# Signed feed-forward with its second layer as seven products of quarters

## The chip, the cores and the metric

One core of one Trainium2 chip runs the whole program: a decoder with two layers, each of self-attention, cross-attention and a feed-forward part. The metric is the device time of one execution in microseconds (us), as the median of the runs. All times in the tables count from the first instruction of the profiled execution.

## The reference

The last of the six stages is the one that changes. Its input x is 2 x 1024 tokens of 256 features; k0, k1 and k2 are boolean matrices of 512 x 1024, 1024 x 1024 and 1024 x 256, and s0, s1, s2 are scalars.

```python
def _L1_ffn_ref(x, k0, k1, k2, s0, s1, s2):
    def _conn_dense(kernel_bool, x):
        w = jnp.where(kernel_bool, jnp.float32(1.0), jnp.float32(-1.0))
        return x @ w
    h = jnp.concatenate([x, -x], axis=-1)
    h = s0 * _conn_dense(k0, h)
    h = jax.nn.relu(h) * 2
    h = s1 * _conn_dense(k1, h)
    h = jax.nn.relu(h) * 2
    h = s2 * _conn_dense(k2, h)
    return h
...
    x = x + _L1_ffn_ref(_layernorm(x, axis=-1), ...)
```

The stage before it is a cross-attention of 8 heads over 154 context rows for every token.

## The kernel before

The program runs stage by stage, with a barrier between stages. Only the last two stages matter here. `headed_attention` (the cross-attention) works in 21 steps on 16 tiles of 128 tokens; step s does a different part of up to five neighbouring tiles. In its spare places it prepares the signed stage: GpSimd turns k1 into +-1 weights in steps 2 to 9 (L3089, between its own `weigh_rest`, L1771, once per step), VectorE and ScalarE take the mean and variance of the first four tiles and split them into a high and a low float16 part (`Rows.low`, `Rows.high`), and TensorE turns them (`Rows.turn`, L861), ScalarE copies the turned tile out of PSUM (`Rows.copy`, L866).

`signed_ffn` works on 4 blocks of 512 tokens. All values are split in two float16 parts, whose products with the +-1 weights are added in float32 in PSUM. A block's layer 1 is 8 chunks of 128 features (4 matmuls of 512 columns each: two parts, two halves of the input), its layer 2 is 8 chunks of 16 matmuls (L3211), and its layer 3 is 4 sums over 16 matmuls of 256 columns (L3217), whose results are scaled and added to x by VectorE (L3161). After each chunk ScalarE writes the high part of the rectified sum (L3181) and VectorE the low part (L3155). The lists `ORDER` and `EARLY` fix the order on all three engines: behind chunks 4, 5 and 6 of layer 2 of a block stand the 8 chunks of layer 1 of the next, behind chunks 0 to 3 the sums of the block before, and behind chunks 2 and 3 the turning of the next block's four tiles, two at a time. GpSimd does nothing but one small power per block (L808).

Each engine takes its own instructions in the order written; a wait holds everything behind it on that engine. A wait on a semaphore stands where the code says `wait_ge`.

Of the kernel before, what the change touches and what calls it, by code (L numbers as in the profile page):

```python
# [17 lines left out]
P = 128  # L18
# [749 lines left out]
class Rows:  # L768
# [4 lines left out]
    def __init__(self, nc, ctx, signals, name, x, room):  # L773
# [8 lines left out]
        self.first = room[:, 1536:2560].bitcast(F16).rearrange("p (c n) -> p c n", c=4)  # L782
        self.s_c, self.var_ready, self.rs_ready, self.nm_ready, self.xh_ready, self.xn_ready, self.turned, self.xT_ready = (
            sem(n) for n in ("s_c", "var_ready", "rs_ready", "nm_ready", "xh_ready", "xn_ready", "turned", "xT_ready"))

    def adopt(self, later):

        self.later = later

    def block(self, b):  # L790
        return self.first if b == 0 else self.later[:, :, BT * (b - 1):BT * b]
# [927 lines left out]
def headed_attention(nc, x, ins, keys, signs, rows, opening):  # L1719
# [8 lines left out]
    with ExitStack() as ctx:  # L1728
# [34 lines left out]
        def _(g):  # L1763
# [12 lines left out]
            for s in STEPS:  # L1776
                weigh_rest(s - 1)
                if s == 2:
                    opening.power(g, 2)
                signs.on_gpsimd(g, own, s)  # L1780
                if s == 1:
                    rows.constants(g)
                if s == 10:
                    rows.power(g, 0)

        @block.vector
        def _(v):
# [41 lines left out]
            for s in STEPS:  # L1829
# [22 lines left out]
                if s in (12, 13):  # L1852
                    rows.low(v, own, s - 12)

        @block.scalar
        def _(a):
# [38 lines left out]
            for s in STEPS:  # L1895
# [1144 lines left out]
class Signs:  # L3040


    def __init__(self, nc, ctx, signals):
# [6 lines left out]
        self.id16, self.made = sb("id16", [P, P], F16), sem("made")  # L3050
# [33 lines left out]
    def on_gpsimd(self, g, own, s):  # L3084
        if 2 <= s < 2 + C1:
# [3 lines left out]
            g.tensor_scalar(self.w[1][:, c], self.k[1][:, c], self.sign2[:, 0:1], self.sign2[:, 1:2], ALU.mult, ALU.add).then_inc(self.expanded[1], 1)  # L3089

# [11 lines left out]
def signed_ffn(nc, x, ins, out, signs, rows):  # L3102


    with ExitStack() as ctx:  # L3105
# [4 lines left out]
        TPB = BT // P  # L3110
        w0, w1, w2 = signs.w
        rows.adopt(sb("xT", [P, 4, BT * (NBLK - 1)], F16))
        h1, h2 = sb("h1", [P, 2, 2, C1, BT], F16), sb("h2", [P, 2, 2, C2, BT], F16)
        BANKS = 4
        psh = ps("psh", [P, BANKS, BT])
        acc = ps("acc", [P, 4, D])
        psx = ps("psx", [P, 2, 1024], F16)
        s_v = sem("s_v")
        layer, hi_done, lo_done, summed, added, stored = (sem(n) for n in ("layer", "hi_done", "lo_done", "summed", "added", "stored"))


        ORDER, PLACE = [(1, 0, n) for n in range(C1)], {}
        EARLY = {4: (0, 1, 2), 5: (3, 4, 5), 6: (6, 7)}
        for b in range(NBLK):
            for n in range(C2):
                ORDER.append((2, b, n))
# [180 lines left out]
```

## Time and profile before

| | us |
|---|---|
| median of 3 runs (1034.52, 1038.59, 1038.72) | 1038.59 |
| profiled execution | 1034.31 |
| its span, first to last instruction | 1032.6 |
| TensorE busy with matmuls | 882.8 (85% of the span) |
| VectorE busy | 747.7 (72%) |
| ScalarE busy | 578.9 (56%) |
| GpSimd busy | 313.8 (30%) |

The page of the profile names the engines PE (TensorE matmul), PEld (its weight loads, which overlap matmuls), DVE (VectorE), ACT (ScalarE), POOL (GpSimd) and SP (the queue that issues DMAs). Busy time of PE is modelled from the starts, and neighbouring matmuls overlap. In the groups, `out<-in` are the program's names for tiles: f_h is an output of a layer (h1 or h2), f_psh and f_acc are PSUM tiles, fs_w the weights, fr_room and f_xT the turned input.

### The profile page before, as it was taken

How to read it: one execution, taken by the hardware profiler on the slowest of the kernel's cores; microseconds unless marked ns; L12 is line 12 of the kernel's file. 1: busy time of each engine (PE TensorE's matmuls, PEld its weight loads, DVE VectorE, ACT ScalarE, POOL GpSimd, SP SyncE). 2: the span in 40 equal slices, each digit the busy share in tenths (PEclk: the TensorE clock that was granted, in tenths of full speed). 3: DMA queues.
4: the chain of work that ended last, by engine and by line, in shares of the span. 5: the costliest groups of instructions: out<-in, count | busy, mean ns of one | idle time of the engine just before them, and what ended most of it. 6: DMA issues, size and time to landing. Idle time of an engine off the chain costs nothing. (4 is left out here: it accounts for less than half of the span.)

```text
span 1032.6 us, 21126 instructions
## 1 busy us (share of the span) xinstructions
PE 882.8 (85%) x8378; PEld 543.6 (53%) x8378; DVE 747.7 (72%) x1416; ACT 578.9 (56%) x1036; POOL 313.8 (30%) x294
## 2 busy tenths in 40 slices
PE   1375978897488799999689999997899988999997
PEld 0122323232256455555356777776799974455554
DVE  7899989834788889887678899875878855344412
ACT  5588789898485555453155555553788844332410
POOL 1043435322265040000266667674234110000000
PEclk9988889799588899999899999998899999999999
DMA  5403232320510030000310000000200000000001
GB/s 147 82 1 52 32 53 32 50 34 1 164 42 2 9 126 1 1 2 1 123 45 2 2 2 2 2 3 1 73 2 1 3 1 1 1 22 1 21 1 41
DMA packets 21600, 30.39 MB, mean 29 GB/s; under 512 B 5936, under 2 KB 17918, under 8 KB 20352
## 3 DMA queue, kind: packets, MB, share of 16 engines
q1 hardware_dynamic: 18752, 26.44, 11.1%
q10 hardware_dynamic: 2752, 2.62, 0.8%
q8 instruction: 67, 1.10, 0.4%
q14 instruction: 29, 0.24, 0.1%
HBM read 18.56 MB, written 2.10 MB: 20 GB/s over the span
## 5 line engine op out<-in xcount | busy, mean ns | idle before, releaser
L589 ACT ACTIVATE t_pT<-t_sc 128x1536 f32<-128x1536 f32 x96 | 136.6, 1455 | 28.2 <-PE t_sc L696 27.9
L696 PE MATMUL t_sc<-t_qk 32*128 32x512 f16 (+3 forms) x1152 | 85.8, 353 | 49.0 <-DMA t_qk<-t_sin_parts 25.7
L269 POOL TENSOR_SCALAR_AFFINE_SELECT t_pT<-t_pT 128x512 f32<-128x512 f32 x64 | 73.4, 1169 | 166.9 <-ACT t_pT L589 166.9
L3155 DVE SCALAR_TENSOR_TENSOR f_h<-f_psh,f_h 128x512 f16<-128x512 f32 x64 | 43.9, 691 | 100.8 <-ACT f_h L3181 100.7
L3211 PE MATMUL f_psh<-f_h,fs_w 128*128 128x512 f16 x512 | 114.4, 379 | 1.5 <-DVE f_h L3155 1.5
L3181 ACT ACTIVATE f_h<-f_psh 128x512 f16<-128x512 f32 x64 | 38.2, 597 | 108.4 <-PE f_psh L3211 108.4
L696 PEld LDWEIGHTS t_sc<-t_qk 32*128 32x128 f16 x1152 | 36.4, 98 | 107.4 <-issue 54.0
L717 PE MATMUL t_ot<-t_pT,t_v 128*17 128x512 f32 (+3 forms) x768 | 81.4, 535 | 12.5 <-DVE t_ou L433 5.5
L2674 POOL TENSOR_SCALAR_AFFINE_SELECT r_att<-r_att 128x1024 f16<-128x1024 f16 x64 | 69.5, 1109 | 66.4 <-DVE r_att L2714 66.3
L3211 PEld LDWEIGHTS f_psh<-f_h,fs_w 128*128 128x128 f16 x512 | 49.8, 98 | 59.0 <-issue 2.0
L1970 PE MATMUL c_pso<-ck_VO,c_pT 128*128 128x256 f16 x480 | 55.0, 273 | 1.4 <-DVE c_pT L1821 1.4
L2714 DVE TENSOR_TENSOR r_att<-r_pss,r_att 128x1024 f16<-128x1024 f32 x32 | 39.1, 1221 | 20.2 <-ACT r_att L2840 20.2
L1970 PEld LDWEIGHTS c_pso<-ck_VO,c_pT 128*128 128x128 f16 x480 | 46.3, 98 | 6.7 <-DVE c_pT L1821 1.6
L1882 ACT ACTIVATE c_pt<-c_pss,c_mx 128x154 f32<-128x154 f32 x128 | 48.5, 415 | 1.1 <-DVE c_mx L1804 1.1
L2320 PE MATMUL m_acc<-gw_down,m_hp 128*128 128x256 f16 x384 | 47.2, 273 | 1.8 <-DVE m_hp L2212 1.4
L2840 ACT CAST r_att<-r_pss 128x1024 f16<-128x1024 f32 x32 | 32.4, 1012 | 28.1 <-PE r_pss L2910 28.0
L2256 ACT ACTIVATE m_sg<-m_psg 128x512 f32<-128x512 f32 x32 | 19.1, 596 | 51.1 <-PE m_psg L2299 51.1
L2936 PE MATMUL r_psv<-ra_w,ra_xT 128*128 128x512 f16 x192 | 46.8, 380 | 1.0 <-ACT r_v L2856 1.0
L2693 POOL TENSOR_TENSOR r_sm<-r_sm,ra_sm 128x16 f32<-128x16 f32 x16 | 46.3, 2896 | 3.6 <-DVE r_sm L2755 2.0
L1771 POOL TENSOR_TENSOR c_pn<-c_pt,c_tot 128x208 f32<-128x208 f32 x16 | 23.1, 1441 | 79.5 <-DVE c_tot L1811 79.5
L717 PEld LDWEIGHTS t_ot<-t_pT,t_v 128*17 128x17 f32 x768 | 17.5, 101 | 51.7 <-issue 37.2
L2320 PEld LDWEIGHTS m_acc<-gw_down,m_hp 128*128 128x128 f16 x384 | 36.9, 98 | 12.4 <-DVE m_hp L2212 2.2
(521 smaller groups left out, 2105.6 us busy)
## 6 DMA issues: line engine op xcount, KB each, us to landing
t_qk<-t_cos_parts SPq DMA_DIRECT2D x24, 128.0 KB, 5.2
t_qk<-t_sin_parts SPq DMA_DIRECT2D x24, 128.0 KB, 6.8
x<-in_x ACTq DMA_DIRECT2D x4, 512.0 KB, 6.4
out_x<-x SPq DMA_DIRECT2D x4, 512.0 KB, 2.9
r_rcos<-in_ret_cos SPq DMA_DIRECT2D x1, 1280.0 KB, 8.8
r_rsin<-in_ret_sin SPq DMA_DIRECT2D x1, 1280.0 KB, 10.5
t_qk<-t_cos_parts SPq DMA_DIRECT2D x16, 64.0 KB, 2.6
gw_raw<-in_gateT SPq DMA_DIRECT2D x1, 1024.0 KB, 7.1
```

The source lines that it names most:

```text
L269: last = g.affine_select(out=blk, in_=blk, compare_op=ALU.is_ge, fill=0.0, base=0, pattern=[[0, 4], [1, P]], channel_multiplier=-1)
L589: a.activation(pT[:, at:at + 3, :].rearrange("p a s -> p (a s)"), sc[s % 2][:], ACT.Exp, scale=CURVE * CURVE / math.sqrt(2 * DH)).then_inc ...
L696: last = t.matmul(sc[s % 2][:, 512 * k + at:512 * k + at + w], qk[r, g % 3, 1, of_k, P * i:P * i + P], qk[r, g % 3, 0, of_q, q0:q0 + w], s ...
L717: last = t.matmul(ot[j][32 * h:32 * h + DH + 1, 512 - w:512], v1[:, b, 4 * c + h, i, :], pT[:, (4 * slot + h) % RING, at:at + w], start=be ...
L1882: last = a.activation(pt[:, q, h, :], pss[:, k, n * CTX:n * CTX + CTX], ACT.Exp, bias=mx[:, q, 3 * k + n:3 * k + n + 1], scale=1.0, accum_ ...
L1970: last = mm(pso[:, 0:D], l, r, start=(n == 0), stop=(n == len(todo) - 1))
L2320: last = mm(acc[:, j, :], hp[:, k, ph_, P * j:P * j + P], dw[:, pw, D * e:D * e + D], start=(e == 0 and j % 2 == 0 and ph_ + pw == 0), sto ...
L2674: last = g.affine_select(out=blk, in_=blk, compare_op=ALU.is_ge, fill=0.0, base=0, pattern=[[0, 8], [1, P]], channel_multiplier=-1)
L2693: g.tensor_tensor(sm[:, q, 2, :], sm[:, q, 1, :], ahead.sm[:, 4, 0:1].broadcast_to((P, HR)), ALU.pow).then_inc(pow_done, 1)
L2936: last = mm(d, l, r, start=(i == 0), stop=(i == len(todo) - 1))
L3155: v.scalar_tensor_tensor(dst[:, 1], psh[:, i % BANKS, :], 0.0, dst[:, 0], ALU.max, ALU.subtract).then_inc(lo_done, 1)
L3211: last = mm(psh[:, i % BANKS, :], l, r, start=(k == 0), stop=(k == len(todo) - 1))
```

## The change

The second layer's weight matrix is cut into 4 quarters of 512 x 512 (halves of the input features by halves of the output features), and a block's input into 4 quarters of 512 features x 256 tokens. Instead of 8 products of quarters, 7 are made, between sums of quarters (Strassen's scheme in Winograd's form). Three sums of weight quarters are made once, and one quarter is overwritten by a difference (`mixture`, by GpSimd, in steps 10 to 13 of the stage before). The sums of token quarters are made for each block by GpSimd in float32, in place (`token_sums`, 8 operations of 128 x 2 x 256 elements per block, in two sets). For them ScalarE writes layer 1's rectified output as float32 (`hf`), beside the float16 high parts of the quarters that are used as they are (`raw_high`); the sums are then split in two float16 parts by ScalarE and VectorE (`token_high`, `token_low`, 128 x 1024 elements each).

Each product is made in two units of 256 output features: 16 matmuls of 256 columns each, into one PSUM bank. p6, p7 and p4 go on in the bank in which p1 stands; between them ScalarE copies the state out as float32 (`keep_p1`, `keep_u2`, `keep_u3`), and VectorE adds p2, p5 or p3 to the copies (`sum_c11`, `sum_c22`, `sum_c12`). The four output quarters are then split as before. The order on every engine is written out: on TensorE a block b is p1 p2 of unit 0, two turns, p1 of unit 1, two turns, p2 of unit 1, p5, sums 0 and 1 of block b-1, p6, tile 0 of layer 1 of block b+1, p5 of unit 1, tile 1, p6, tile 2, p7, tile 3, p7, tile 4, p4, tile 5, p3, tile 6, p4, tile 7, sums 2 and 3 of block b-1, p3 of unit 1. The turned tiles have two places instead of one for each block. The rows of block 1 are normalised in the stage before (steps 13 to 18), those of blocks 2 and 3 in blocks 0 and 1. The output leaves in pieces of two tiles instead of four. New buffers lie in rooms of stages that are over (`keys.VO`, `keys.kT`, `keys.wq16`, `early.room`, and the boolean weights).

The core of the diff:

```diff
+        if self.alternate:
+            return self.later if b % 2 else self.first
...
+                if s in (10, 14):
+                    rows.power(g, (s - 10) // 4)
...
+                if s in (13, 14):
+                    v.wait_ge(x_done, 2 * s - 20)
+                    rows.statistics(v, own, 2 * s - 22, 2 * s - 20)
+                if s == 14:
+                    rows.spread(v, own, 1)
+                if s == 16:
+                    rows.offsets(v, 1)
+                if s in (17, 18):
+                    rows.low(v, own, s - 15)
...
+                if s in (17, 18):
+                    rows.high(a, s - 15)
...
+        todo = ((self.mix[:, 0], a(1, 0), a(1, 1), ALU.add), (self.mix[:, 1], self.mix[:, 0], a(0, 0), ALU.subtract),
+                (a(1, 0), a(0, 0), a(1, 0), ALU.subtract), (self.mix[:, 2], a(0, 1), self.mix[:, 1], ALU.subtract))
+        g.wait_ge(self.expanded[1], C1)
+        wait(g, self.mixed, n)
+        to, left, right, op = todo[n]
+        g.tensor_tensor(to, left, right, op).then_inc(self.mixed, 1)
...
+        rows.adopt(old[:, 8192:10240].rearrange("p (c n) -> p c n", c=4), True)
...
+        z, y = [ps(f"z{i}", [P, BT]) for i in range(2)], [ps(f"y{i}", [P, BT]) for i in range(2)]
+        pw, pl = ps("w", [P, BT]), ps("l", [P, BT])
+        acc, psx = ps("acc", [P, 2, D]), ps("psx", [P, 2, 512], F16)
...
+        CHUNKS = (0, 4, 1, 5, 2, 6, 3, 7)
...
+                    sp.wait_ge(added, t + 2)
+                    t0 = P * (t % (2 * TPB))
+                    sp.dma_start(out[b // 2][t0:t0 + 2 * P].rearrange("(t p) d -> p t d", p=P), x[:, t:t + 2, :]).then_inc(stored, 16)
...
+            def token_sums(b, i):
+                f, s_ = hf[i]
+                b11, b12, b21, b22 = f[:, :, 0:HT], f[:, :, HT:BT], s_[:, :, 0:HT], s_[:, :, HT:BT]
+                g.wait_ge(f_done, 8 * b + 4 * i + 4)
+                own.link(g.tensor_tensor(b11, b12, b11, ALU.subtract))
+                g.tensor_tensor(b12, b22, b12, ALU.subtract).then_inc(t_made, 1)
+                g.wait_ge(t_made, 4 * b + 2 * i + 1)
+                own.link(g.tensor_tensor(b22, b22, b11, ALU.subtract))
+                g.tensor_tensor(b21, b21, b22, ALU.subtract).then_inc(t_made, 1)
+                g.wait_ge(t_made, 4 * b + 2 * i + 2)
...
+            token_sums(0, 0)
+            token_sums(0, 1)
+            for b in range(NBLK):
+                if b + 2 < NBLK:
+                    rows.power(g, b + 2)
+                if not closing(b):
+                    token_sums(b + 1, 0)
+                    token_sums(b + 1, 1)
...
+            def token_low(b, i, j):
+                v.wait_ge(t_high, 4 * b + 2 * i + j + 1)
+                v.tensor_tensor(tm[:, b % 2, 1, i, j], hf[i][j], tm[:, b % 2, 0, i, j], ALU.subtract).then_inc(t_split, 1)
...
+            def sum_c12(u):
+                v.wait_ge(u2_kept, u + 1)
+                v.wait_ge(p3_done, u + 1)
+                v.tensor_tensor(second_kept[u % 2], second_kept[u % 2], halves(y[u % 2]), ALU.add).then_inc(c12_sum, 1)
...
+            def low(u, half, side, high, split, src):
+                v.wait_ge(high, u + 1)
+                v.scalar_tensor_tensor(out_part(u, half, side, 1), src, 0.0, out_part(u, half, side, 0), ALU.max, ALU.subtract).then_inc(split, 1)
...
+            for b in range(NBLK):
+                u0, u1 = UNITS * b, UNITS * b + 1
+                if b:
+                    sum_c12(u0 - 1)
+                    low_c12(u0 - 1)
+                token_low(b, 1, 0)
+                sum_c11(u0)
+                token_low(b, 1, 1)
+                low_c11(u0)
+                sum_c11(u1)
+                low_c11(u1)
+                if b:
+                    add(b - 1, 0, acc)
+                if b + 2 < NBLK:
+                    rows.statistics(v, own, TPB * (b + 2), TPB * (b + 3))
+                if not closing(b):
...
+                low_c12(u0)
+                if not closing(b):
+                    raw_low(b + 1, 6)
+                    token_low(b + 1, 0, 1)
+                low_c21(u1)
+                if not closing(b):
+                    raw_low(b + 1, 7)
+                if b + 2 < NBLK:
+                    rows.offsets(v, b + 2)
+                    rows.low(v, own, 2 * (b + 2))
+                if b:
+                    add(b - 1, 2, acc)
+                if b + 2 < NBLK:
+                    rows.low(v, own, 2 * (b + 2) + 1)
+            last = NBLK - 1
+            sum_c12(UNITS * NBLK - 1)
+            low_c12(UNITS * NBLK - 1)
...
+            def raw_high(b, i):
+                n, (src, dst) = CHUNKS[i], raw_parts(b, i)
+                a.wait_ge(tiled, 8 * b + i + 1)
+                if b:
+                    a.wait_ge(t_split, 4 * (b - 1) + 2 * (n % HC // 2) + 2)
+                a.activation(hf[n % HC // 2][n // HC][:, n % 2, :], tile_bank(b, i)[:], ACT.Relu).then_inc(f_done, 1)
+                if b >= 2:
+                    a.wait_ge(p3_done, UNITS * (b - 1))
+                a.activation(dst[:, 0], src, ACT.Relu).then_inc(r_high, 1)
...
+            def token_high(b, i, j):
+                a.wait_ge(t_made, 4 * b + 2 * i + j + 1)
+                if b >= 2:
+                    a.wait_ge(p4_done, UNITS * (b - 1))
+                a.copy(tm[:, b % 2, 0, i, j], hf[i][j]).then_inc(t_high, 1)
+
+            def copy_rows(t):
+                a.wait_ge(rows.turned, t + 2)
+                rows.copy(a, t, psx[:, 0])
+                rows.copy(a, t + 1, psx[:, 1])
...
+            def keep(u, done, into, freed, kept):
+                a.wait_ge(done, u + 1)
+                wait(a, freed, u - 1)
+                a.copy(into[u % 2], halves(z[u % 2])).then_inc(kept, 1)
...
+            for b in range(NBLK):
+                u0, u1 = UNITS * b, UNITS * b + 1
+                if b:
+                    high_c12(u0 - 1)
+                keep_p1(u0)
+                token_high(b, 1, 0)
+                token_high(b, 1, 1)
+                if not closing(b):
+                    copy_rows(TPB * (b + 1))
+                high_c11(u0)
+                keep_p1(u1)
+                if not closing(b):
+                    copy_rows(TPB * (b + 1) + 2)
+                high_c11(u1)
+                keep_u2(u0)
+                if not closing(b):
+                    raw_high(b + 1, 0)
+                    raw_high(b + 1, 1)
...
+                high_c22(u1)
+                high_c21(u0)
+                if not closing(b):
+                    raw_high(b + 1, 5)
+                    token_high(b + 1, 0, 0)
+                high_c12(u0)
+                if not closing(b):
+                    raw_high(b + 1, 6)
+                    token_high(b + 1, 0, 1)
+                high_c21(u1)
+                if not closing(b):
+                    raw_high(b + 1, 7)
+                if b + 2 < NBLK:
+                    rows.high(a, 2 * (b + 2))
+                    rows.high(a, 2 * (b + 2) + 1)
+            high_c12(UNITS * NBLK - 1)
...
+            def product(u, bank, first, left, right, done):
+                into = halves(bank)
+                for i in range(2):
+                    m = P * (2 * (u % UNITS) + i)
+                    for c in range(HC):
+                        for part in range(2):
+                            last = mm(into[:, i, :], left[:, c, m:m + P], right(u // UNITS % 2, part, c), start=(first and i + c + part == 0),
+                                      stop=(c == HC - 1 and part == 1), skip_group_check=True)
...
+            def p2(u):
+                t_.wait_ge(r_split, 8 * (u // UNITS) + 8)
+                wait(t_, c11_sum, u)
...
+            def p5(u):
+                t_.wait_ge(t_split, 4 * (u // UNITS) + 3)
+                wait(t_, c12_sum, u - 1)
...
+            def p6(u):
+                t_.wait_ge(t_split, 4 * (u // UNITS) + 4)
+                t_.wait_ge(p1_kept, u + 1)
...
+            def turn(t):
+                rows.turn(t_, t, psx[:, t % 2], signs.id16, t - t % 2)
...
+            for b in range(NBLK):
+                u0, u1 = UNITS * b, UNITS * b + 1
+                t = TPB * (b + 1)
+                p1(u0)
+                p2(u0)
+                if not closing(b):
+                    turn(t)
+                    turn(t + 1)
+                p1(u1)
+                if not closing(b):
+                    turn(t + 2)
+                    turn(t + 3)
+                p2(u1)
```

Of what is left out, `p1`, `p7`, `p4` and `p3` are like `p6`, each with the waits named above; `raw_low` is like L3155 with one input in PSUM; in `headed_attention` nothing else changes.

## Rows read from the trace of the kernel before

**Rows 1.** The chain that ended last, its end: start, us, engine, what, count.
```profile
962.54 24.17 PE f_psh L3211 x112
...
1017.88 6.56 PE f_acc L3217 x60
...
1024.46 0.88 DVE x L3161 x2
```

**Rows 2.** Busy time in a stretch: length, then PE, PEld, DVE, ACT, POOL, clock.
```profile
920.00:940.00 20.00, 20.00 (x96) 9.08 (x94) 8.89 (x15) 7.58 (x13) 0.00 (x0) 1.00 0.08 27
```

**Rows 3.** The matmuls of two lines: count, ns min/median/max, first and last start.
```profile
L3211 PE MATMUL f_psh<-f_h,fs_w x512: 376/379/379, 862.9 to 1017.5; 128*128 128x512 f16 x171
...
L3217 PE MATMUL f_acc<-fs_w,f_h x256: 272/273/273, 901.7 to 1024.6; 128*128 128x256 f16 x128
```

**Rows 4.** ScalarE in order of time: start us, us, engine, line, operation.
```profile
796.35 1.12 ACT L3099 ACTIVATE fs_w<-fs_k 128x1024 f16<-128x1024 uint8 x1
...
873.90 1.08 ACT L843 ACTIVATE fr_room<-x,fr_sm 128x256 f16<-128x256 f32 x2
...
877.80 1.07 ACT L866 COPY f_xT<-f_psx 128x512 f16<-128x512 f16 x2
```

**Rows 5.** VectorE in order of time.
```profile
796.33 1.23 DVE L1814 TENSOR_TENSOR c_pn<-c_pt,c_tot 128x1024 f32<-128x1024 f32 x1
...
867.13 0.69 DVE L3155 SCALAR_TENSOR_TENSOR f_h<-f_psh,f_h 128x512 f16<-128x512 f32 x1 [4.42 <-ACT f_h L3181]
867.74 1.39 DVE L817 BATCH_NORM_STATS2 fr_st<-x 128x6 f32<-128x256 f32 x4
...
871.40 0.73 DVE L849 TENSOR_SCALAR fr_room<-x,fr_sm 128x256 f32<-128x256 f32 x2
...
872.22 0.91 DVE L854 TENSOR_TENSOR fr_room<-fr_room 128x256 f16<-128x256 f32 x2
```

**Rows 6.** GpSimd in order of time.
```profile
372.02 1.29 POOL L2450 TENSOR_TENSOR gw_raw<-gw_raw 128x512 f32<-128x512 f32 x1 [7.77 <-DMA gw_raw<-in_L_attn_g_w]
```

**Rows 7.** The start of the signed stage, in order of time.
```profile
854.28 1.02 PE L3211 MATMUL f_psh<-fr_room,fs_w 128*128 128x512 f16 x4 [1.75 <-PEq L51]
...
855.34 0.60 ACT L3181 ACTIVATE f_h<-f_psh 128x512 f16<-128x512 f32 x1 [2.19 <-PE f_psh L3211]
...
862.85 1.45 PE L3211 MATMUL f_psh<-f_h,fs_w 128*128 128x512 f16 x6 [1.50 <-DVE f_h L3155]
```

**Rows 8.** VectorE and GpSimd beside each other in earlier stages.
```profile
327.26 1.00 DVE L826 TENSOR_SCALAR mr_sm<-mr_sm 128x4 f32<-128x4 f32 x1
...
373.41 1.68 DVE L2212 TENSOR_TENSOR m_hp<-m_h,m_hp 128x512 f16<-128x512 f32 x1
...
375.01 2.28 DVE L2526 SCALAR_TENSOR_TENSOR ra_wo<-gw_raw,ra_wo 128x1024 f16<-128x1024 f32 x1
...
376.18 2.25 POOL L2451 TENSOR_TENSOR gw_raw<-gw_raw 127x512 f32<-127x512 f32 x1
...
381.96 0.68 DVE L2212 TENSOR_TENSOR m_hp<-m_h,m_hp 128x512 f16<-128x512 f32 x1
```

**Rows 9.** The stage before: GpSimd's steps and the last copy, in order of time.
```profile
748.20 1.19 POOL L3089 TENSOR_SCALAR fs_w<-fs_k,fs_sign 128x1024 f16<-128x1024 uint8 x1
...
796.38 1.57 POOL L1771 TENSOR_TENSOR c_pn<-c_pt,c_tot 128x208 f32<-128x208 f32 x1 [4.65 <-DVE c_tot L1811]
...
803.73 1.57 POOL L1771 TENSOR_TENSOR c_pn<-c_pt,c_tot 128x208 f32<-128x208 f32 x1 [4.82 <-DVE c_tot L1811]
...
852.57 0.58 ACT L866 COPY fr_room<-c_psq 128x512 f16<-128x512 f16 x1 [4.22 <-PE c_psq L861]
```

**Rows 10.** DMA issues: tiles, queue, count, KB each, us to landing.
```profile
out_x<-x SPq DMA_DIRECT2D x4, 512.0 KB, 2.9
```

**Rows 11.** Busy time in two stretches, columns as in rows 2.
```profile
712.00:716.00 4.00, 1.06 (x7) 0.71 (x8) 2.47 (x5) 0.77 (x2) 0.18 (x1) 0.82 0.00 0
716.00:720.00 4.00, 2.55 (x12) 1.52 (x10) 0.42 (x1) 0.00 (x0) 0.00 (x0) 0.50 0.00 0
```

More of the change, by code:

```diff
@@ L3110, in signed_ffn @@
         TPB = BT // P
+        HT, HC, UNITS = BT // 2, C1 // 2, 2
         w0, w1, w2 = signs.w
[L3112 to L3119, printed above, removed]
@@ L3163, in _ @@
-            for i, (layer_, b, n) in enumerate(ORDER):
-                rest(i)
-                if layer_ == 2:
-                    if n == 4 and b:
-                        add(b - 1)
-                    if b + 1 < NBLK:
-                        if n == 0:
-                            rows.variances(v, own, b + 1)
-                        if n == 1:
-                            rows.offsets(v, b + 1)
-                        if n in (1, 2):
-                            rows.low(v, own, 2 * (b + 1) + n - 1)
@@ new lines, in keep_p1, with keep_u2, keep_u3, high @@
+            def keep_p1(u):
+                keep(u, p1_done, first_kept, c11_split, p1_kept)
+            def keep_u2(u):
+                keep(u, p6_done, second_kept, c12_split, u2_kept)
+            def keep_u3(u):
+                keep(u, p7_done, third_kept, c22_split, u3_kept)
+            def high(u, half, side, ready, done, src):
+                a.wait_ge(ready, u + 1)
+                wait(a, summed, TPB * (u // UNITS - 1))
+                a.activation(out_part(u, half, side, 0), src, ACT.Relu).then_inc(done, 1)
@@ new lines, in high_c11, with high_c12, high_c21, high_c22 @@
+            def high_c11(u):
+                high(u, 0, 0, c11_sum, c11_high, first_kept[u % 2])
+            def high_c12(u):
+                high(u, 0, 1, c12_sum, c12_high, second_kept[u % 2])
+            def high_c21(u):
+                high(u, 1, 0, p4_done, c21_high, halves(z[u % 2]))
+            def high_c22(u):
+                high(u, 1, 1, c22_sum, c22_high, third_kept[u % 2])
+            for i in range(C1):
+                raw_high(0, i)
+            token_high(0, 0, 0)
+            token_high(0, 0, 1)
@@ new lines, in p4, with p3, sums @@
+            def p4(u):
+                t_.wait_ge(u3_kept, u + 1)
+                product(u, z[u % 2], False, signs.quarter(1, 1), token4, p4_done)
+            def p3(u):
+                t_.wait_ge(c22_sum, u + 1)
+                product(u, y[u % 2], False, signs.mix[:, 2], raw22, p3_done)
+            def sums(b, j, bank):
+                if j % 2 == 0:
+                    wait(t_, added, TPB * b + (j if bank is acc else 0))
+                for k, c in enumerate((0, 1, 4, 5, 2, 3, 6, 7)):
+                    if j % 2 == 0 and k in (0, 4):
+                        u, side = UNITS * b + k // 4, j // 2
+                        t_.wait_ge((c11_split, c12_split)[side], u + 1)
+                        t_.wait_ge((c21_split, c22_split)[side], u + 1)
+                    for part in range(2):
+                        last = mm(bank[:, j % 2, :], h2[:, b % 2, part, c, P * j:P * j + P], w2[:, c, :],
+                                  start=(j % 2 == 0 and k + part == 0), stop=(k == C2 - 1 and part == 1), skip_group_check=True)
+                last.then_inc(summed, 1)
@@ L3248, in program @@
+            last = NBLK - 1
+            sums(last, 0, acc)
+            sums(last, 1, acc)
+            sums(last, 2, pl[:].rearrange("p (j d) -> p j d", j=2))
+            sums(last, 3, pl[:].rearrange("p (j d) -> p j d", j=2))
 def program(nc, ins, out):
```

278 lines of the change are left out of this document (191 added, 87 removed).

## The prediction, made before the changed kernel had run

> **What bounds the kernel now.** I read the chain of waits first, then the busy time by stretch, then the prices. The chain's last 170 us are TensorE alone: matmuls of L3211 and L3217 in turn, and only the last adds behind them [rows 1]. The stretch table says why: TensorE is busy 20.00 of 20 us, VectorE 8.9, ScalarE 7.6, GpSimd nothing, at clock 1.00 [rows 2]. The signed stage runs from its first matmul at 854.28 to the last at 1024.46, 170.2 us. So TensorE's columns are the stage's time, and the other three engines have some 11 us of every 20 free. The change spends this free time, and the question is whether it spends it in the right places.
>
> **Part 1, the products.** A 512-column matmul costs 24.17/112 = 0.2158 us, a 256-column one 6.56/60 = 0.1093 [rows 1] (their busy figures of 379 and 273 ns in rows 3 are longer because matmuls overlap). Layer 2 has 512 of the first kind [rows 3], 110.5 us. Afterwards: 7 products x 16 matmuls x 2 units x 4 blocks = 896 of 256 columns, 98.0 us. Saved 12.5 us. Layer 1 (128 matmuls), the third layer (256 of L3217, rows 3) and the turns stay the same. One product is 1.75 us, a layer-1 tile 0.86, two sums 3.5, two turns 0.45; a block is then 39.3 us of TensorE instead of 42.4.
>
> **Part 2, what the other engines get.** Prices by row: ScalarE reading PSUM, 512 wide, 0.60 (I take a pitch of 0.57, since copies of this width follow each other at 0.53); 1024 from SBUF 1.12; copying two turned tiles 1.07; two normalised tiles 1.09 [rows 4, 7]. VectorE: 512 wide 0.69 (the next one starts 0.61 later), 1024 wide 1.23, two tensor_scalar 0.73, two tensor_tensor of 256 some 0.7 to 0.9 [rows 5]. GpSimd: a float32 tensor_tensor of 512 elements 1.29 [rows 6], which is the size of each token sum. Per block ScalarE gets 8 float32 copies and 8 high parts of layer 1 (about 8.4), 4 token parts (4.4), 6 keeps (3.4), 8 output parts (5), copies and normalisations (4.3): 25.5 of 39.3. VectorE about 25, GpSimd 8 x 1.35 = 10.8. No engine passes TensorE in sum. What decides is order: every engine is a queue, and the new chains cross it.
>
> The Trainium skill ("GPSIMD Engine Reference", section 3.1 on elementwise operations) gives 4497 ns for a GpSimd float32 tensor_tensor of 2048 elements, a quarter of which, as an estimate, is 1.12 us. By that figure the opening's eight token sums would end 1.4 us earlier than by the row's 1.29.
>
> **The opening.** I count from the first matmul; ScalarE starts 1.06 later [rows 7]. Each tile now takes it two activations (0.57 + 0.57 or 0.36), so the eighth ends at 9.35, and the first product can start when the seventh is split, 8.75; before, layer 2 started at 8.57 (862.85, rows 7). Cost 0.2. GpSimd starts its sums after four tiles, at 4.75, and needs eight operations of 1.35 with their waits: 15.5 at the earliest. TensorE meanwhile runs two products, two turns, one product: done at 14.45. The next turn waits until ScalarE has copied the first two, and in ScalarE's queue these copies stand behind the token part that needs the eighth sum: 15.55 + 1.05 + 1.07 = 17.8. Stall 3.35 us.
>
> **The lock.** Here VectorE also does tensor_tensor with both inputs in SBUF (token low parts), beside GpSimd's. The trace shows such a pair: L2212 takes 0.68 alone and 1.68 with a GpSimd sum running; GpSimd's L2451, of the size that took 1.29, takes 2.25 behind VectorE's L2526 of 1024, which itself took 2.28; even a tensor_scalar of 4 elements took 1.00 [rows 6, 8]. They exclude each other for whole instructions and alternate. VectorE operations with one PSUM input are not held. With two token low parts of 1.15 and then a third between GpSimd's sums, the eighth ends at 18.7 and the copies at 20.9: stall 6.5.
>
> **The block ends.** Template of a block, from its first product at 0: turns at 3.5 and 5.7, p6(u0) ends 14.9, tile 0 15.8, tile 3 23.6, tile 7 34.0, end 39.3. From there ScalarE and VectorE pass work to and fro (keeps, c22, c21, tiles, tokens, c12): by the prices tile 7's high part ends at 37.8, its split at 38.5, against 34.0 for its matmuls. Behind it VectorE still has, in blocks 0 and 1, the normalisation of tiles for block b+2: offsets, two times 1.4 us, and 0.8 for an add: end 41.45 (block 0, no add) or 42.25. Only then comes sum_c12 of the last unit, and then, strictly in this order, on ScalarE high_c12, keep_p1, two token parts, copy_rows: 0.65 + 0.65 + 0.6 + 2.1 + 1.07 = 5.1 us after VectorE is done. TensorE reaches the turn that waits for copy_rows 5.7 us into the next block. Block 0 ends at 35.8 in the template (it has no sums of a previous block), so block 1's turn is wanted at 41.5 and, with 1.1 us for the late split, set free at 46.7: 5.2 us lost in all. Block 2's is wanted at 45.0 and free at 47.5: 2.5. Block 3 has no turns but waits 0.3 for c11. Sum with no lock: 3.35 + 5.2 + 2.5 + 0.3 = 11.4.
>
> With the lock: GpSimd starts the second token sums of block b+1 at about 37.9, so its four operations stand exactly beside VectorE's offsets, tensor_scalars and tensor_tensors, each of which has to let one pass. The normalisation ends at 46.05 and 46.85 instead. Block 1 then waits for the turned tiles' inputs (41.1 to 44.3) and again for copy_rows (46.9 to 51.25), with the late split 9.75 us; block 2 7.0; block 3 1.05. Sum 6.5 + 9.75 + 7.0 + 1.05 = 24.3. The rows of the lock are strict, so I take 22 of the span 11.4 to 24.3.
>
> **The stage before.** GpSimd gets four operations on 2048 float16 elements at its steps 10 to 13, behind weigh_rest, which ends at 797.95 [rows 9] and comes again 7.4 us later. No row has this size: from below twice the 1.19 of a one-input operation of 1024 [rows 9], 2.4; from above four times the 1.29 of 512 float32 elements, 5.2. I take 5.2, because it has two inputs too. It fits into the 5.8 us between, so it costs nothing; at 1 us more each, it would hold VectorE's 1024-wide operation with two SBUF inputs at the head of each step, and TensorE up to 4 us behind it. VectorE gets statistics and spread at steps 13 and 14 (2.1 us, in a stretch with some 1.3 free per step): 0.3. The normalisation of block 1's last tiles comes at step 18, behind ScalarE's copy at 852.57 to 853.15 [rows 9]: one pair of 1.09, then VectorE's last 0.35. The barrier moves by 1.5. In sum +1.8 (0 to 6).
>
> **The end.** Before, four adds follow the last matmul (1.66 us, first 0.88 in rows 1) and 512 KB go out in 2.9 us [rows 10]. After, two adds and half the bytes: -0.8 and, no row showing 256 KB of this kind, between 0 and -1.45, I take -0.7. Together -1.5.
>
> **The clock.** From 712 to 716 TensorE was busy 1.06 of 4 us, and the granted clock there was 0.82 and in the next 4 us 0.50, that is, it fell from 2.4 to 1.2 GHz [rows 11]. Stalls of 4 to 6.5 us in blocks 0, 1 and 2 look like that. After one, work at half clock loses half its time; the low level filled 716 to 720 there, with TensorE at work for 2.55. Three stalls, 0 to 10 us, taken 3.
>
> **Sum.** -12.5 + 0.2 + 22 + 1.8 - 1.5 + 3 = +13.0 us on the profiled execution's 1034.3, 1047.3. The median shown is 4.3 higher, 1038.6, with two of three runs there and one at 1034.5; on the median it is 1051.6. I say 1050.
>
> **Rivals.**
> A, equal: the lock costs little and the clock holds. -12.5 + 0.2 + 11.4 + 1.8 - 1.5 = -0.6: 1038. For it: GpSimd's queue might be done before VectorE's own long run; one-PSUM-input operations are free of it. Against: the start of the token sums and of the normalisation are both set by tile 7.
> B, faster: the saved columns come through, -12.5 + 0.2 - 1.5 and 2 of stalls, 1027. Its place is TensorE's wait on copy_rows. It decides if copy_rows is done by 5.7 us into the block, for which ScalarE and VectorE would have to reach tile 7's split at 33, 5 us sooner than my queue. For it: both are only two thirds busy. Against: the hand-overs, each priced by a row.
> C, far slower: the half clock lasts through a block's first part after every stall, and the mixtures delay weigh_rest too: +13 - 3 + 10 + 4, 1061.
> D, the products of quarters don't reach 0.1094 because weights change at every matmul: but L3217 changes them too and has that pace; +0.02 each would be 18 us. Held under C.
>
> **How the numbers follow.** Forecast 0.50, A 0.22, B 0.13, C with D 0.15. A measurement of this kernel can tell about 0.5%, 5.2 us, from no change: faster is under 1033.4, same to 1043.8. The forecast's own range 1044 to 1057 leaves a little for same. Range 1035 to 1062: it leaves out B and the far end of C. Faster 0.14, same 0.24, slower 0.62.
>
> **What would show it.** Right: TensorE idle in the signed stage in three places, each ended by ScalarE's copies of turned tiles, 3 to 7 us each; GpSimd tensor_tensors of 512 elements at 1.3 alone and over 2 in company; VectorE's small tensor_scalars over 1 us at the block ends; first signed matmul near 856; products at 1.75 us. Wrong: TensorE idle under 5 us in the stage (then B), the clock at 1.00 throughout with stalls near 11 (A), or the headed stage's steps longer than 7.4 us (C).

## The result: 1.2% slower

The changed kernel takes 1049.45 us (median of 4 runs, 1049.01 to 1049.79) against 1036.75 for the kernel before (4 runs beside it, 1034.52 to 1038.72): ratio 1.0123, 95% interval 1.0095 to 1.0151, +12.7 us by the medians. The forecast was 1050. The profiled execution took 1049.79 with a span of 1048.0, which is 15.4 more than the span before. Of these, 1.3 lie ahead of step 10 of the attention, in code that the change doesn't touch; over the twelve traces of this case that point varies by 4.8 us.

The page's busy times of the kernel after:

```profile
PE 886.3 (85%) x8762; PEld 584.6 (56%) x8762; DVE 789.2 (75%) x1456; ACT 617.3 (59%) x1108; POOL 375.4 (36%) x330
```

No engine came near its limit: VectorE got 41.5 us, ScalarE 38.4 and GpSimd 61.6 more. The loss is in the order of events. TensorE's waits in the signed stage after (start us, us, operation, in brackets the idle time before it and what ended it):

```profile
858.07 1.02 PE L3456 MATMUL f_l<-fr_room,fs_w 128*128 128x512 f16 x4 [3.10 <-PEq L51]
879.56 1.01 PE L864 MATMUL f_psx<-fs_id,fr_room 128*128 128x128 f16 x8 [6.10 <-ACT ck_VO L869]
910.55 1.92 PE L3465 MATMUL f_w<-ck_VO,fs_w 128*128 128x256 f16 x16 [0.78 <-DVE ck_VO L3234]
913.66 0.40 PE L864 MATMUL f_psx<-fs_id,fr_room 128*128 128x128 f16 x4 [1.18 <-DVE fr_room L857]
915.06 0.40 PE L864 MATMUL f_psx<-fs_id,fr_room 128*128 128x128 f16 x4 [1.01 <-DVE fr_room L857]
921.06 1.01 PE L864 MATMUL f_psx<-fs_id,fr_room 128*128 128x128 f16 x8 [3.86 <-ACT fr_room L869]
966.58 1.01 PE L864 MATMUL f_psx<-fs_id,fr_room 128*128 128x128 f16 x8 [4.64 <-ACT ck_VO L869]
```

L864 is the turn, L869 its copy on ScalarE, L857 the last step of the normalisation, L3465 a product. The first line is the barrier ahead of the stage. With 0.79 in the opening the waits inside the stage are 18.4 us; before there was one, 1.5. The chain's end shows the products at their price, 1.75 us each, and the last add of the kernel (the chain of waits: start, us, engine, what):

```profile
1025.83 1.75 PE f_y L3465 x16
1027.57 1.75 PE f_z L3465 x16
1029.32 3.49 PE f_acc L3534 x32
...
1041.58 0.48 DVE x L3274
```

The clock behind the barrier, in block 0 and in block 2, by stretches (length, then PE, PEld, DVE, ACT, POOL, granted clock; the waits of block 1 were followed by 0.50 too):

```profile
858.00:864.00 6.00, 5.93 (x20) 2.41 (x21) 1.54 (x3) 3.42 (x8) 0.00 (x0) 0.72 0.02 4
864.00:870.00 6.00, 5.21 (x36) 3.19 (x34) 3.98 (x6) 5.47 (x12) 5.60 (x5) 1.00 0.00 0
874.00:880.00 6.00, 0.44 (x5) 0.47 (x6) 3.16 (x4) 3.50 (x6) 3.29 (x2) 0.70 0.00 0
880.00:884.00 4.00, 4.00 (x27) 3.06 (x25) 0.90 (x2) 1.49 (x3) 0.00 (x0) 0.60 0.00 0
966.00:972.00 6.00, 5.42 (x30) 4.05 (x31) 2.80 (x4) 2.76 (x6) 0.00 (x0) 0.51 0.00 0
```

From 880 to 884 TensorE counts as fully busy and does less: 27 matmuls, some of them turns of 128 columns, where 37 of 256 columns would fit at full pace. The granted clock is 0.60 over this stretch, since the low level ends within it. After block 2's wait it is at 0.51, that is 1.2 GHz.

From first to last matmul the signed stage takes 183.48 us after and 170.58 before. A version below (v2) has this work at clock 1.00 and takes 161.91 with 4.83 of waits: the work alone is 157.1. So the stage after is 157.1 + 18.4 of waits + 8.0 that are left over, which I put down to the half clock, and the stage before 169.1 + 1.5. The same split gives −0.3 for e_v2_writes_only below, so it is good to some 0.3 us.

### The profile page after: what moved, and what is told of

The parts are those of the page before. It is cut to its first block and busy times, and to the rows that moved or that the text cites. A ratio compares the mean times of both kernels' runs of the same rounds, so it can differ in the third digit from the quotient of the medians.

```text
span 1048.0 us, 22181 instructions
## 1 busy us (share of the span) xinstructions
PE 886.3 (85%) x8762; PEld 584.6 (56%) x8762; DVE 789.2 (75%) x1456; ACT 617.3 (59%) x1108; POOL 375.4 (36%) x330
## 3 DMA queue, kind: packets, MB, share of 16 engines
q10 hardware_dynamic: 2752, 2.62, 0.9%
## 5 line engine op out<-in xcount | busy, mean ns | idle before, releaser
L696 PE MATMUL t_sc<-t_qk 32*128 32x512 f16 (+3 forms) x1152 | 89.4, 366 | 45.7 <-DMA t_qk<-t_sin_parts 25.1
L717 PEld LDWEIGHTS t_ot<-t_pT,t_v 128*17 128x17 f32 x768 | 17.8, 103 | 52.6 <-issue 39.3
L1774 POOL TENSOR_TENSOR c_pn<-c_pt,c_tot 128x208 f32<-128x208 f32 x16 | 24.1, 1506 | 59.2 <-DVE c_tot L1814 59.2
L2924 PEld LDWEIGHTS r_pss<-r_qkT 32*128 32x128 f32 x512 | 31.9, 191 | 13.4 <-issue 11.6
L3375 ACT ACTIVATE f_h<-fs_k 128x512 f16<-128x512 f32 x24 | 15.1, 631 | 40.7 <-DVE fs_k L3253 25.7
L2924 PE MATMUL r_pss<-r_qkT 32*128 32x128 f32 x512 | 38.1, 288 | 0.0
L2861 ACT COPY r_qkT<-r_ptr 128x512 f32<-128x512 f32 x32 | 18.8, 588 | 30.6 <-PE r_ptr L2998 30.6
```

The lines of the kernel that those rows point to most:

```text
L696: last = t.matmul(sc[s % 2][:, 512 * k + at:512 * k + at + w], qk[r, g % 3, 1, of_k, P * i:P * i + P], qk[r, g % 3, 0, of_q, q0:q0 + w], s ...
L717: last = t.matmul(ot[j][32 * h:32 * h + DH + 1, 512 - w:512], v1[:, b, 4 * c + h, i, :], pT[:, (4 * slot + h) % RING, at:at + w], start=be ...
L2924: last = mm(pss[:, j, P * g:P * g + P], qkT[r, q, 1, g, :], qkT[r, q, 0, g, :], start=(g == 0), stop=True, skip_group_check=True)
```

## Why block 0's turn waits

GpSimd, VectorE and ScalarE of the kernel after, in order of time:

```profile
868.13 1.27 POOL L3215 TENSOR_TENSOR ck_wq<-ck_wq 128x512 f32<-128x512 f32 x1
869.48 2.13 POOL L3211 TENSOR_TENSOR f_hf<-f_hf 128x512 f32<-128x512 f32 x1
870.51 2.18 DVE L3238 TENSOR_TENSOR f_tm<-ck_wq,f_tm 128x1024 f16<-128x1024 f32 x1
...
875.24 2.13 POOL L3215 TENSOR_TENSOR f_hf<-f_hf 128x512 f32<-128x512 f32 x1
877.40 1.04 ACT L3351 CAST f_tm<-f_hf 128x1024 f16<-128x1024 f32 x1 [2.50 <-POOL f_hf L3215]
878.35 1.06 ACT L869 COPY ck_VO<-f_psx 128x512 f16<-128x512 f16 x2
...
909.17 1.26 POOL L3211 TENSOR_TENSOR f_hf<-f_hf 128x512 f32<-128x512 f32 x1 [6.96 <-ACT f_hf L3342]
910.48 2.79 DVE L852 TENSOR_SCALAR fr_room<-x,fr_sm 128x256 f32<-128x256 f32 x2
910.51 1.27 POOL L3212 TENSOR_TENSOR f_hf<-f_hf 128x512 f32<-128x512 f32 x1
```

A token sum takes 1.27 alone and 2.13 beside VectorE's L3238, whose two inputs are both in SBUF and which itself takes 2.18 instead of 1.22. At the block's end two tensor_scalars (L852), which read one tile from SBUF, take 2.79 instead of 0.73 beside two of these sums, which keep their 1.27 there. ScalarE's copy of the turned tiles (878.35) has its data since the turns of 871.10; it stands behind the token part (877.40), which waits for GpSimd's eighth sum. TensorE's turn at 879.56 waits for that copy. This is the predicted chain: eighth sum 18.7 after the first matmul by the prediction, 19.3 measured (877.37 − 858.07), of which 1.7 come from the opening's half clock. In e_mix_writes, whose opening ran at full clock, it ended 17.6 after the first matmul.

## The experiments

Each ran beside the kernel before on the same chip (medians 1035.66, 1035.70 and 1036.07 in the three batches). "Waits" are TensorE's in the signed stage, without the barrier's; "clock loss" is the stage less its waits, less 157.1, less any added matmuls at 0.1093. The traces are one execution each, and the opening alone moves a stage by 1.7 us from one to another, as told below.

| kernel | median us (runs) | ratio to before | stage | waits | clock loss |
|---|---|---|---|---|---|
| after | 1049.45 (4) | 1.0123 [1.0095, 1.0151] | 183.48 | 18.4 | 8.0 |
| e_fill | 1044.49 (5) | 1.0073 [1.0037, 1.0109] | 179.27 | 7.9 | 3.8 |
| e_copies_first | 1047.33 (2) | 1.0113 [1.0048, 1.0179] | 178.02 | 16.0 | 5.0 |
| e_writes_only | 1040.47 (8) | 1.0049 [1.0031, 1.0067] | 170.95 | 9.2 | 4.7 |
| e_short_sums | 1033.54 (8) | 0.9984 [0.9962, 1.0005] | 166.12 | 5.5 | 3.5 |
| e_rows_mid | 1040.58 (5) | 1.0038 [1.0019, 1.0057] | 174.33 | 12.1 | 5.1 |
| e_mix_writes | 1045.70 (2) | 1.0101 [1.0075, 1.0127] | 181.97 | 16.7 | 8.2 |
| v1 | 1029.84 (5) | 0.9948 [0.9935, 0.9962] | 163.60 | 4.8 | 1.7 |
| v2 | 1026.19 (4) | 0.9912 [0.9897, 0.9927] | 161.91 | 4.8 | 0 |
| v3 | 1025.70 (6) | 0.9909 [0.9888, 0.9929] | 160.92 | 3.8 | 0 |
| e_v2_writes_only | 1023.86 (2) | 0.9888 [0.9857, 0.9919] | 160.00 | 3.2 | −0.3 |

### The clock: more matmuls in the same wait

```
-                p1(u1)
+                p1(u1, 3 if not closing(b) else 1)
```

> In blocks 0, 1 and 2 product 1 of unit 1 is computed three times instead of once, so that 96 more matmuls (10.5 us of columns) stand where TensorE waits for the copies of the turned tiles (6.1, 3.9 and 4.6 us in the changed kernel). The result is unchanged. The signed stage of the changed kernel runs 183.3 us from its first to its last matmul. If the granted clock falls because of these waits, it stays at 1.00 in blocks 0 to 2 here and the stage takes 177 to 180 us although more is computed. If the clock has nothing to do with the waits, the stage takes 183 to 184 (the matmuls are hidden in the waits); if the waits are not what I think, up to 194.

The kernel computes 96 matmuls more (10.5 us of TensorE) and its stage is 4.2 us shorter. The third line is the stretch of block 2's wait, which stood at 0.51:

```profile
874.00:880.00 6.00, 3.38 (x33) 2.84 (x31) 3.14 (x3) 3.49 (x6) 3.40 (x2) 0.96 0.00 0
880.00:886.00 6.00, 6.00 (x47) 4.99 (x46) 2.26 (x4) 2.25 (x5) 0.00 (x0) 0.75 0.02 3
966.00:972.00 6.00, 6.00 (x58) 5.38 (x56) 1.99 (x4) 1.62 (x4) 0.00 (x0) 1.00 0.00 0
```

The waits shrank by the added work exactly (18.4 − 7.9 = 10.5), so what was gained is clock: the loss fell from 8.0 to 3.8. What is left is the opening's 1.7, the same in both traces, and a wait of 2.62 in block 0, after which the clock still fell; it was expected to stay at 1.00 there.

The length of a wait doesn't settle by itself whether the clock falls. The barrier's wait was 3.1 us in eight of the kernels here. In six of them the first product began 9.54 us after the first matmul, with the clock at 0.50 from about 859 to 862.5. In two it stayed at 1.00 and the product began at 7.87, though the code up to there is the changed kernel's in e_copies_first, and in e_mix_writes it differs only in the stage before:

```profile
861.54 1.02 PE L3456 MATMUL f_l<-fr_room,fs_w 128*128 128x512 f16 x4 [3.11 <-PEq L51]
...
869.41 1.91 PE L3465 MATMUL f_z<-ce_room,fs_w 128*128 128x256 f16 x16 [0.80 <-DVE ce_room L3234]
```

A wait of 3.08 in block 0 of e_copies_first left the clock at 1.00 as well.

### Is it the place of the copies alone?

```
                 keep_p1(u0)
+                copy_rows(TPB * (b + 1))
                 token_high(b, 1, 0)
                 token_high(b, 1, 1)
-                copy_rows(TPB * (b + 1))
```

> Only ScalarE's order at the start of a block changes: the copies of the first two turned tiles stand ahead of the two token parts instead of behind them. If the stall is one of this queue order, TensorE's wait at the second pair of turns goes (6.1, 3.9, 4.6 us), and is replaced in block 0 by a wait for the token parts at product 5 or 6 some 5 us earlier than now; stage 183.3 -> 173 to 176. If it is the sums themselves, or the normalisation ahead of c12, that come too late, the wait only moves to products 5 and 6 and the stage stays above 180.

Neither bound was met: 178.0. Of the 5.5 us that the stage is shorter, 1.7 are the opening's clock, which this edit can't have changed. Taking the copies out from behind the token parts brings block 0's wait from 6.10 to 3.08, and then another engine's queue holds the same work. TensorE's waits there:

```profile
878.78 1.91 PE L3465 MATMUL f_w<-ck_VO,fs_w 128*128 128x256 f16 x16 [3.08 <-DVE fs_k L3243]
...
919.02 3.57 PE L3465 MATMUL f_w<-ck_VO,fs_w 128*128 128x256 f16 x16 [2.20 <-DVE fs_k L3243]
```

L3243 is sum_c11, which stands in VectorE's queue behind token_low. By medians two runs don't tell this kernel from the changed one; in the trace its waits are 2.4 us less, and block 0's moved from the turn to a product.

### The lock: token sums that read nothing

```
-                own.link(g.tensor_tensor(b11, b12, b11, ALU.subtract))
...
+                own.link(g.memset(part, 1.0))
+                own.link(g.memset(part[:, 0:1], 1.0))
+                last = g.memset(part[:, 1:2], 1.0)
```

> Each of GpSimd's token sums is replaced by three memsets of its output, some 1.2 to 1.3 us together and thus as long as a sum alone, but with nothing read; the token sums themselves are left out. If GpSimd and VectorE hold each other up only where both read, the 2.13 us operations go, VectorE's two tensor_scalars of 2.79 us at the end of block 0 fall to 0.73, block 0's stall of 6.1 shrinks to 2.5 to 3.5 and those of blocks 1 and 2 by 1.5 to 2.5 each: stage 183.3 -> 174 to 178. If the lock is not the reason (queue order and latency alone), the stage stays at 182 to 184.

GpSimd and VectorE of this kernel at the same place, in order of time:

```profile
868.38 1.23 DVE L3243 TENSOR_TENSOR f_tm<-ck_kT,f_tm 128x1024 f16<-128x1024 f32 x1 [0.23 <-ACT f_tm L3356]
868.79 0.53 POOL L3212 MEMSET f_hf<- 128x512 f32 x1
869.37 0.31 POOL L3213 MEMSET f_hf<- 128x256 f32 x1
```

GpSimd is as long busy (0.53 + 0.31 + 0.31 and gaps for each sum), but only writes, and VectorE's two-input operation keeps its 1.23 beside it. (L3243 here is L3238 of the changed kernel.) The stage is 12.5 us shorter, more than expected: 9.2 of waits and 3.3 of clock. The waits that stay are 3.31 (block 0), 3.67 and 1.42, each ended by L869; without the lock the prediction had 3.35, 5.2 and 2.5. What the Trainium skill states ("SBUF — State Buffer", section "Who interferes with whom"), that a VectorE instruction with two SBUF inputs contends with a GpSimd instruction that reads SBUF and not with one that only writes it, agrees with both traces: 2.18 against 1.23.

> GpSimd's token sums are made over 1/16 of their columns; the rest is left out. Both their latency and the lock go. Block 0's stall should fall to 0 to 1.5 us; in blocks 1 and 2 what is left is the order alone: normalisation, c12, first product kept, token parts, copies, by my queue walk 2.5 to 4 us each. Stage 183.3 -> 168 to 173. If the order had no part in it, 162 to 165.

The sums cover 1/16 of their columns here, so time and lock both go. Block 0's wait is gone, blocks 1 and 2 keep 3.60 and 1.14; stage 166.1, less than the 168 expected, and the median isn't told from the kernel before. Even with nearly free token sums the stage is only 4.5 us shorter than before, of the 12.0 that the columns save: 9.0 are in waits and clock, 1.7 of them the opening's clock and 0.8 a wait in the opening. The other 6.5 are what the queue order costs by itself, waits and the clock behind them.

### The block's end: normalisation in its middle

```
+                if b + 2 < NBLK:
+                    rows.statistics(v, own, TPB * (b + 2), TPB * (b + 3))
+                    rows.spread(v, own, b + 2)
+                    rows.offsets(v, b + 2)
+                    rows.low(v, own, 2 * (b + 2))
+                    rows.low(v, own, 2 * (b + 2) + 1)
                 if b:
                     add(b - 1, 0, acc)
```

> The normalisation of block b+2's tiles moves, on VectorE and ScalarE, from the end of block b, where GpSimd makes token sums, to the middle of block b, where GpSimd is idle (ahead of the adds and of the first keep of p6). If blocks 1 and 2 lose their time because this work is held up by GpSimd there and holds up c12 in its turn, TensorE's waits for the normalised tiles (1.18 and 1.01 us) go and the waits for copies fall from 3.9 and 4.6 us to under 1.5; block 0's 6.1 stays. Stage 183.5 -> 174 to 177. If it is only the order of copies behind the token parts on ScalarE, the copies still come 2 to 3 us late in both blocks and the stage stays above 178.

The stage is 174.3, as expected; block 2's wait and those for the normalised tiles are gone, and the two tensor_scalars of L852 are back at 0.73. Block 1's turn still waits 3.34 where under 1.5 was expected: GpSimd's last sum there takes 2.12 beside VectorE's token_low, and the copies stand behind it. A new wait of 1.10 stands at a tile of layer 1 in block 0. The normalisation was the work that met GpSimd's second group of token sums.

### The stage before: mixtures that only write

```
-        g.tensor_tensor(to, left, right, op).then_inc(self.mixed, 1)
+        g.memset(to, 1.0).then_inc(self.mixed, 1)
```

> GpSimd's four operations on weights in the stage before (4.06 us each) become memsets of the same tiles (1.8 us, nothing read); the sums of weight quarters are left out. In the changed kernel the interval between GpSimd's operations L1774 at the steps was 7.35, 7.38, 7.86, 8.51 us against 7.35, 7.38, 7.37, 7.38 before. If the lock with VectorE's normalisation of block 0 in steps 12 and 13 made these 1.6 us, the two intervals fall to 7.4 to 7.5 and the signed stage starts 1.5 us earlier relative to the first L1774. If it was VectorE's own added statistics, the second interval (8.51) keeps 0.8 to 1.1 of its excess.

A mixture takes 4.06 us after. Two of the four, and GpSimd's step heads around them, in the kernel after, and VectorE beside them:

```profile
813.98 4.06 POOL L3120 TENSOR_TENSOR fs_w<-fs_w 128x2048 f16<-128x2048 f16 x1
817.23 1.28 DVE L852 TENSOR_SCALAR fr_room<-x,fr_sm 128x256 f32<-128x256 f32 x2
...
820.30 1.57 POOL L1774 TENSOR_TENSOR c_pn<-c_pt,c_tot 128x208 f32<-128x208 f32 x1 [2.27 <-DVE c_tot L1814]
821.84 4.05 POOL L3120 TENSOR_TENSOR fs_mix<-fs_w,fs_mix 128x2048 f16<-128x2048 f16 x1
824.60 1.76 DVE L852 TENSOR_SCALAR fr_room<-x,fr_sm 128x256 f32<-128x256 f32 x2
...
828.81 1.57 POOL L1774 TENSOR_TENSOR c_pn<-c_pt,c_tot 128x208 f32<-128x208 f32 x1 [2.92 <-DVE c_tot L1814]
```

The steps that these close last 7.86 and 8.51 instead of 7.38. With writes only they last 7.38 and 7.96 (L1774 at 813.00, 820.38, 828.34). So of 1.6 us that the two steps lose, 1.03 go with the mixtures: the two tensor_scalars of L852 take 1.28 and 1.76 beside them and 0.73 each time beside the writes. The 0.58 that stay are put down to VectorE's added statistics (L820, 0.74 us in this step), which no run takes out. The signed stage starts 1.0 us earlier, counted from the L1774 ahead of the first mixture, where 1.5 was expected.

### Three versions with other orders and the same work

v1 keeps every operation and changes queue orders alone:

```
 TensorE: p1(u0) p2(u0) p1(u1) p2(u1) | turn, turn | p5(u0) | turn, turn | p5(u1) | ...
 ScalarE: keep_p1(u0), token_high(1,0), high_c11(u0), keep_p1(u1), token_high(1,1)*, copy_rows, high_c11(u1), copy_rows
 VectorE: sum_c11(u0), token_low(1,0), low_c11(u0), sum_c11(u1), token_low(1,1), low_c11(u1);
          the normalisation as in e_rows_mid
 (* behind the first copy_rows in block 0)
```

> All orders together: normalisation in mid-block as above; the turns behind product 2 and product 5 of unit 0 instead of behind products 2 and 1; product 5 of unit 1 ahead of the sums; on ScalarE the first copies ahead of the last token part in block 0; on VectorE sum_c11 ahead of the token part. No operation is added or left out. By the queue walk the stalls fall to 3 to 5 us in all (block 0: 2 to 3) and the clock stays at 1.00 after the first 10 us: stage 183.5 -> 161 to 165, the kernel 1027 to 1032. If the other engines' total work were the limit instead of their order, the waits move to later products and the stage stays above 172.

Stage 163.6, ratio 0.9948, as expected: from 1.2% slower to 0.5% faster than before. The largest wait left is 2.30. The orders were changed together; what one gives alone was tried only in e_copies_first and e_rows_mid.

v2 also moves the normalisation of block 1's last pair from step 18 behind the barrier:

```
-                if s in (17, 18):
-                    rows.low(v, own, s - 15)
+                if s == 17:
+                    rows.low(v, own, 2)
...
+            rows.low(v, own, 3)
             for i in range(C1):
                 raw_low(0, i)
```

> v1, and the normalisation of block 1's last two tiles moves from the last step of the stage before, behind which the barrier stands, to the start of the signed stage, where ScalarE waits 1 us for the first tile anyway. The signed stage starts 1.0 to 1.5 us earlier relative to the last matmuls of the stage before and is as long as in v1 or up to 0.5 us longer. If the barrier was not held by this work, nothing changes.

TensorE's barrier wait is 1.59 instead of 3.11, so the stage starts 1.5 us sooner after the last c_pso matmul; and the clock doesn't fall: the same opening that stood at 0.72 is at 1.00, another 1.7 us. The three kernels with a barrier wait of 1.59 all kept the clock, but so did two of the eight with 3.1, so it isn't shown that every execution gains this 1.7. v2's waits in the stage, from its order of time:

```profile
857.19 1.02 PE L3458 MATMUL f_l<-fr_room,fs_w 128*128 128x512 f16 x4 [1.59 <-PEq L51]
865.06 1.91 PE L3467 MATMUL f_z<-ce_room,fs_w 128*128 128x256 f16 x16 [0.80 <-DVE ce_room L3234]
...
885.38 1.04 PE L3458 MATMUL f_l<-ck_VO,fs_w 128*128 128x512 f16 x4 [2.30 <-DVE ce_room L3234]
903.75 1.92 PE L3467 MATMUL f_w<-ck_VO,fs_w 128*128 128x256 f16 x16 [0.79 <-DVE ck_VO L3234]
```

and the stretch of its opening; over block 2, from 940 to 980, the clock is 1.00 too:

```profile
857.00:863.00 6.00, 5.81 (x27) 2.67 (x28) 4.01 (x9) 5.83 (x13) 1.39 (x2) 1.00 0.01 4
```

> v2 with the token sums replaced by memsets as in the experiment on the changed kernel, where this took 12.5 us off the signed stage (183.5 -> 171.0). The token sums are left out. If the new order has taken VectorE's and TensorE's waits out of the lock's way, only 0 to 2 us are left to gain: stage 161.9 -> 160 to 162. If the lock costs what it cost and v2's gain has another source, the stage falls by 5 us or more, to 157 or less.

The lock that cost the changed kernel 12.5 us of its stage costs v2 1.9 (161.91 against 160.00): the operations that held each other are all still there, but of what TensorE waits for only three short waits, of 0.42, 0.52 and 0.79 us, go with the lock.

v3 moves the mixtures to steps 10, 11, 14 and 15 and puts the block's second normalised pair behind the first tile:

> v2 with two more moves. GpSimd's operations on weights go from steps 10 to 13 of the stage before to steps 10, 11, 14 and 15, away from VectorE's normalisation of block 0 in steps 12 and 13: the intervals of L1774 there should fall from 7.86 and 8.52 us to 7.4 and 7.9 to 8.0. In block b the second pair of normalised tiles goes behind the first tile of layer 1 on both engines: in v2 TensorE waited 2.3 us for that tile's low part in block 0. The wait should fall under 1 us. In sum 1.5 to 3.0 us less than v2: 1023 to 1025. If the order was not the reason for either, the time stays at 1026.

The trace shows 1.0 us less in the stage (a wait of 2.30 becomes 1.31, where under 1 was expected), and 0.5 less in the stage before: the two steps are back at 7.37 and 7.96, but a later one takes 7.75 instead of 7.12. The runs, 1025.70 against 1026.19, don't separate it from v2 and miss the 1023 to 1025 expected. v2 and v3 beat both kernels: 0.9% faster than before, and by the ratios 2.1% faster than the changed kernel.

## Why the prediction held

| step | predicted | measured |
|---|---|---|
| products, 256 columns instead of 512 | −12.5 | −12.0 |
| opening, splits of layer 1 | +0.2 | −0.7 (a wait of 0.79 for one of 1.50) |
| block 0, turn behind ScalarE's copies | 6.5 | 6.10 |
| block 1, turn inputs, then copies | 9.75 | 6.8 |
| block 2 | 7.0 | 4.64 |
| block 3 | 1.05 | 0 |
| taken for the four | 22 | 17.6 |
| half clock | +3 | +8.0 |
| stage before | +1.8 | +2.5 |
| end | −1.5 | −1.3 |

The measured rows add up to 14.1, which is the 15.4 of the spans less the 1.3 ahead of step 10.

**Right.** The mechanism and the places: a saving in columns that comes in full, and ScalarE's copies of turned tiles as the end of three waits. Block 0 was walked queue by queue and came within 0.4 us; without the lock the walk gave 3.35 where 3.31 was measured. Here too both ends of the difference were about 1 us late: at full clock the first product starts at 7.87 and not 8.75, and the eighth sum ends at 17.6 and not 18.7. The price of the token sums (1.29 by the row, 1.27 measured), the 2.13 and 2.18 of the locked pair and the 2.1 us for 256 KB out (taken at 2.2) follow from the rows.

**Off in size, and cancelling.** The walk of the block's end was too long by 1.5 (block 1) and 1.1 (block 2) even without the lock, and the lock itself was sized at 4.55 and 4.5 there where it takes 3.2 in each. Part of the 1.5 can be read in e_short_sums: tile 7's split ended 34.2 us after block 0's first product, where the template, less the pair of sums ahead of it, gives 35.0, and the five operations from sum_c12 to the copies took 4.7 and not 5.1, because each starts before its forerunner's row is over. The template for block 0 has a slip as well: it takes one pair of sums off 39.3 and lets the block end at 35.8, but block 0 has neither pair, so it is 32.3, which e_short_sums shows (870.90 to 903.20). The slip makes both the time at which block 1's turn is wanted and the time at which it is free 3.5 too late, so it drops out of the stall. So the term "22 for the stalls" is 4.4 too large. The term "clock, 3" is 5.0 too small: the low level came with all three stalls and cost 1.5 to 2.6 us each time, and it came with the barrier too, 1.7 us, which the sum didn't count. The lock costs clock as well as time: 3.3 of its 12.5. The two errors cancel (25 against 25.6), so the total deserves less credit than its mechanism. The median has luck of its own: the sum gave 1051.6 on a kernel before at 1038.59, and 1050 was said without a term for the 1.6; four runs put that kernel at 1036.75, and +13.0 on this is 1049.8.

**Not as said.** The mixtures "cost nothing": they are shorter than the 5.2 taken (4.06) and fit, yet 1.03 us is lost, since VectorE's tensor_scalars beside them are held. The opening costs nothing: the first product starts earlier after the first matmul than layer 2 did before (7.87 against 8.57 at full clock). The barrier, 1.5 taken, moved by 1.35, and VectorE's statistics, 0.3 taken, cost 0.58. A step near 841 became 0.5 shorter.

**Rivals.** A and B are false for the kernel as written. With the orders changed B's saving nearly comes: v2 is 9.5 us under the kernel before, where B said 11.8, for the case that copy_rows is early enough. C fell: the low level ended within some 5 us after the end of each wait, and GpSimd sat idle 0.8 to 2.9 us before each weigh_rest (L1774) that follows a mixture, so the mixtures didn't hold it by their length. Its sign, steps longer than 7.4 us, did show in two steps (7.86 and 8.51), by 1.6 us and not by C's 4. D fell too (1.75 us a product).

Open: why the step near 841 gets shorter, and why the clock fell behind a barrier wait of 3.1 us in six kernels and not in two.

## What to carry to other kernels

When work leaves the bounding engine for engines with free time, walk their queues: name each copy that the bounding engine waits for and what stands ahead of it in its queue. An order that never mattered (copies behind a part that a slow engine feeds) turns a 12 us saving into a 12 us loss, and changing only the order gives it back; the lock's cost, too, is decided by who is queued behind the held operation. A wait on TensorE can cost more than its length: the stretches at the low clock behind the longer waits here cost another 1.5 to 2.6 us each, behind the barrier too, but they didn't come every time.

## What the runs showed of the hardware

- TensorE's granted clock fell with waits of 3.86, 4.64 and 6.10 us in the changed kernel and of 2.62 in e_fill, with two waits of 1.97 and 2.20 in block 1 of e_copies_first, and with a barrier wait of 3.1 in six kernels of eight; it stayed at 1.00 after the other two, after a wait of 3.08, after 2.30 (v1, v2) and after 1.59. It cost 8.0 us in all in the changed kernel, more than expected. 96 useless matmuls put into the waits gave back 4.2.
- Beside a VectorE tensor_tensor with two SBUF inputs, GpSimd's reading operation of 1.27 took 2.13. VectorE's pairs of tensor_scalars, with one tile from SBUF, were held too: 2.79 beside token sums, 1.28 and 1.76 beside mixtures, 0.73 alone. A GpSimd operation that only writes neither held nor was held (0.53 and 1.23).
- GpSimd's float16 tensor_tensor of 2048 elements took 4.06 us, less than four float32 ones of 512 (4 x 1.27).
